# Gated cross-attention with a ternary feed-forward: two subtractions per tile moved from VectorE to GpSimd in the hand-ordered opening, exponential biases made for two banks at a time, dummy matmuls cut into smaller pieces, and the lists of all engines reordered

## What is computed

```python
# x, ctx: 32 tiles of 128 rows x 512; 16 heads of 32
q = rms_norm(linear(layernorm(x), q_w, q_b), norm_q_w)
k = rms_norm(linear(ctx, k_img_w, k_img_b), norm_k_w)     # 128 rows: all of them are "image" rows,
v = linear(ctx, v_img_w, v_img_b)                          # so the text branch is empty
x = x + tanh(g_xattn) * linear(softmax(q k^T / sqrt(32)) v, o_w, o_b)
w1, w2 = ternary(W_fc), ternary(W_proj)                    # sign(w) * group mean |w|, groups of 64, or 0
h = relu(layernorm(x) @ w1.T) ** 2                         # 2048 wide
x = x + tanh(g_ffn) * (rms_norm(h) @ w2.T)
```

## Time and profile before

| | |
|---|---|
| median of 3 runs | 920.4 us (919.91 to 922.21) |
| the profiled execution | 920.16 us, span in the profile 918.3 us |
| busy share of the span | PE 96%, ACT 87%, DVE 77%, POOL 61%, PE weight loads 58% |
| mean granted PE clock | 0.985 of full |
| first maximum (L1640) of tiles 0 to 6 | at 30.28, 56.10, 78.90, 105.53, 134.69, 159.44 and 184.42 us |

### The profile page before, as it was taken

How to read it: one execution, slowest core, us unless ns; L and a number is a source line. 1 busy time by engine, 2 the same in 40 slices (tenths; PEclk the granted TensorE clock), 3 DMA queues, 4 the chain that set the end, 5 groups by cost and what they waited for, 6 DMA issues and landing times.

```text
span 918.3 us, 22391 instructions
## 1 busy us (share of the span) xinstructions
PE 878.6 (96%) x7536; PEld 532.6 (58%) x7633; DVE 710.3 (77%) x1546; ACT 798.8 (87%) x1608; POOL 560.5 (61%) x616
## 2 busy tenths in 40 slices
PE   8687899999999999999999999999999999999998
PEld 5333465555665666656556666555566665556675
DVE  7999999878788787878788787878788787867301
ACT  6998999899899888889989888899898888989573
POOL 3222255776676766667666766667677666656476
PEclk9797899999999999999999999999999999999999
DMA  9958665676676676667666866566667656654501
GB/s 370 208 121 198 147 163 103 100 138 123 127 119 125 127 139 109 106 119 128 127 116 130 132 117 102 119 128 127 120 131 130 116 104 120 124 107 79 82 12 47
DMA packets 319890, 115.78 MB, mean 126 GB/s; under 512 B 305184, under 2 KB 305440, under 8 KB 318240
## 3 DMA queue, kind: packets, MB, share of 16 engines
q1 hardware_dynamic: 319776, 114.34, 63.6%
HBM read 30.67 MB, written 8.39 MB: 43 GB/s over the span
## 4 chain that ended last, share of the span: by engine, by line
PE 76%; ACT 4%; issue 2%; DMA 1%; POOL 1%; DVE 1%; SPq 0%; POOLq 0%; ACTq 0%; DVEq 0%
PE mix_pair L594 11%; PE up_pair L578 10%; PE up_pair L579 10%; PE mix_pair L593 8%; PE score_pair L532 5%; PE score_pair L531 5%; PE score_pair L533 5%; PE mix_pair L531 3%; PE mix_pair L532 3%; PE mix_pair L533 3%; PE score_ps L532 2%; PE score_ps L531 2%; PE score_ps L533 2%; PE score_pair L662 2%; ACT big L1030 1%
## 5 line engine op out<-in xcount | busy, mean ns | idle before, releaser
L578 PE MATMUL up_pair<-ft_all,w 128*128 128x256 f16 x960 | 215.9, 274 | 1.5 <-ACT h_all L1024 0.6
L579 PE MATMUL up_pair<-ft_all,w 128*128 128x256 f16 x960 | 216.0, 274 | 0.0
L2185 POOL TENSOR_TENSOR big<-h_all,big 128x512 f16<-128x512 f32 x128 | 154.2, 1205 | 57.0 <-ACT h_all L1033 38.9
L594 PE MATMUL mix_pair<-w,big 128*128 128x512 bf16 x464 | 175.9, 379 | 7.0 <-issue 4.1
L2195 POOL TENSOR_TENSOR h_all<-h_all,hh_sb 128x512 f32<-128x512 f32 x112 | 143.3, 1279 | 28.1 <-ACT hh_sb L1051 26.7
L593 PE MATMUL mix_pair<-w,big 128*128 128x512 bf16 x383 | 145.2, 379 | 0.2 <-POOL big L2185 0.2
L2140 POOL TENSOR_TENSOR ln_rstd<-ln_in,minus_half 128x1 f32<-128x1 f32 x64 | 46.0, 718 | 112.5 <-issue 90.8
L578 PEld LDWEIGHTS up_pair<-ft_all,w 128*128 128x128 bf16 x960 | 94.0, 98 | 18.4 <-DMA ft_all<-x_rows 1.2
L579 PEld LDWEIGHTS up_pair<-ft_all,w 128*128 128x128 bf16 x960 | 94.1, 98 | 15.8
L1093 ACT ACTIVATE score_ps<-score_ps,exp_bias,exp_scale 128x128 f32<-128x128 f32 x256 | 94.2, 440 | 0.0
L1093 ACT ACTIVATE score_pair<-score_pair,exp_bias,exp_scale 128x128 f32<-128x128 f32 x256 | 93.5, 429 | 0.3 <-DVE exp_bias L1644 0.2
(11 more groups left out here) (236 smaller groups left out, 2304.1 us busy)
## 6 DMA issues: line engine op xcount, KB each, us to landing
x_sb<-in_x SPq DMA_DIRECT2D x32, 256.0 KB, 3.2
ctx_sb<-in_ctx_t SPq DMA_DIRECT2D x32, 256.0 KB, 3.3
out<-out_sb SPq DMA_DIRECT2D x31, 256.0 KB, 3.5
big<-in_w_proj_t SPq DMA_DIRECT2D x4, 1024.0 KB, 5.6
big<-in_w_fc_t SPq DMA_DIRECT2D x2, 1024.0 KB, 7.6
pt<-p_rows SPq DMA_TRANSPOSE x128, 3.2
big<-in_wq_t SPq DMA_DIRECT2D x1, 1024.0 KB, 4.9
big<-in_wk_t SPq DMA_DIRECT2D x1, 1024.0 KB, 7.4
```

What stands on the lines that cost most here:

```text
L578: nc.tensor.matmul(dst[:, half], w, ft[i][:, c, :], start=(c == 0), stop=False)
L579: last = nc.tensor.matmul(dst[:, half], w, ft[i][:, C + c, :], start=False, stop=(c == C - 1))
L594: last = nc.tensor.matmul(dst[:, cols], ht_lo[i][:, row], w2[:, m, cols], start=False, stop=(m == M - 1))
L2185: nc.gpsimd.tensor_tensor(ht_lo[i][:, rows], h_sb[k % 3][:, :], ht_hi[i][:, rows], ALU.subtract).then_inc(hlo_ready, 1)
```

## The change

`x_lo` and `normed_lo` become POOL steps for x_lo(1) to x_lo(7) and normed_lo(0) to normed_lo(4). From tile 6's slot on, DVE does them as before. In the opening, `score_tops` (four times maximum, bias) gives way to `score_tops_by_two` (twice: maximum, maximum, one bias instruction of 8 columns). The dummies: 22 `warm_first` become 16. The 51 `warm` stay 51 but come in calls of 1 or 2 instead of 4 to 6: before scores(1) 9 instead of 14, and 5 between scores(1) and scores(2); between scores(2) and scores(3) 17 instead of 21; between scores(3) and scores(4) 8 instead of 12; between scores(4) and scores(5) 12 instead of 4. All lists of the opening are reordered. The diff, cut to its core:

```diff
@@ SP @@
+            load_context(0, 0)
             load_x(0, 0)
+            load_small(vb_col, v_b, vb_in_ready)
             load_weight(0, wq_t)
-            load_context(0, 0)
...
@@ PE @@
-            warm_first(14)
+            warm_first(5)
+            warm_first(5)
+            spread_context(0, up_b)
             first_rows()
-            spread_context(0, up_b)
-            warm_first(8)
+            warm_first(3)
+            warm_first(3)
...
             ternary_pair(0)
+            scores(0)
             constant_row()
-            scores(0)
+            next_keys(0)
             next_queries(0)
-            next_keys(0)
+            next_values(0)
             values(0)
...
             ffn_up(0, 3, 3, up_ps, 1)
-            next_context(4)
-            ternary_half(31)
-            ffn_down(0, range(0, 4), mix_ps)
+            ffn_up(1, 0, 0, up_b)
+            scores(5)
             ffn_down(0, range(4, 12), mix_ps)
-            scores(5)
             project_out(4)
-            ffn_up(1, 0, 0, up_b)
             square_sums(0)
@@ ACT @@
+            relu(0, 2, 0, up_ps)
             exps(3, 0)
             exps(3, 1)
...
@@ DVE @@
+            def score_tops_by_two(t):
+                dve.wait_ge(s_done, t + 1)
+                if t == 0:
+                    dve.wait_ge(exp_scale_ready, 1)
+                for b in (0, 2):
+                    n, heads = 4 * t + b, slice(4 * b, 4 * b + 8)
+                    need(dve, bias_ready, n - 2)
+                    for i in range(2):
+                        nc.vector.tensor_reduce(m_top[:, 4 * (b + i):4 * (b + i) + 4],
+                                                score_ps[b + i][:, :].rearrange("p (u k) -> p u k", k=P), AX.X,
+                                                ALU.max).then_inc(top_ready, 1)
+                    dve.wait_ge(top_ready, n + 2)
+                    need(dve, exp_ready, n - 2)
+                    nc.vector.tensor_scalar(exp_bias[:, heads], m_top[:, heads], minus_scale[:, :], LOG_P_SCALE,
+                                            ALU.mult, ALU.add).then_inc(bias_ready, 2)
...
-            weight_lo(2)
-            score_tops(0)
+            context_lo(1, 1)
             ternary_clip(0)
             ternary_mask(0)
+            score_tops_by_two(0)
+            weight_lo(2)
             probs_lo(0, 0)
+            constant_row()
             probs_lo(0, 1)
-            context_lo(1, 1)
-            constant_row()
-            weight_lo(3)
+            next_rows(2)
+            k_out(1)
             probs_lo(0, 2)
             probs_lo(0, 3)
@@ POOL @@
+            def x_lo(t):
+                pool.wait_ge(xhi_ready, t)
+                need(pool, xt_in, 16 * (t - 1))
+                nc.gpsimd.tensor_tensor(x_rows[:, 1, :], xn[:, :], x_rows[:, 0, :], ALU.subtract).then_inc(xlo_ready, 1)
+
+            def normed_lo(t):
+                pool.wait_ge(fhi_ready, t + 1)
+                need(pool, ft_in, 16 * t)
+                nc.gpsimd.tensor_tensor(x1_rows[:, 1, :], x1n[:, :], x1_rows[:, 0, :], ALU.subtract).then_inc(flo_ready, 1)
...
             x_norm(1, 1)
+            x_lo(1)
             norm_product()
...
             x1_norm(0, 0)
-            q_norm(2)
+            normed_lo(0)
             x_norm(3, 3)
+            x_lo(3)
...
             k_rms_of(6)
+            rows_plus_constant(4, 0)
+            hidden_lo(1, 0, 0)
             q_norm(6)
```

More of the change, by code:

```diff
@@ L1948, in _ @@
-            q_lo(2)
-            attention(1, 1)
-            ternary_clip(4)
-            ternary_clip(5)
-            ternary_mask(4)
-            ternary_final(3)
-            context_top(3)
-            attention_lo(1)
+            ternary_final(2)
+            probs_lo(1, 2)
+            probs_lo(1, 3)
+            k_out(2)
+            ternary_clip(4)
+            x1_out(0, 0)
+            q_out(2)
+            next_context(3)
+            x1_stats(0, 0)
+            k_lo(2)
+            attention(1, 0)
@@ L1956, in _ @@
+            attention(1, 1)
+            q_lo(2)
+            ternary_mask(4)
+            ternary_signed(4)
+            ternary_final(3)
+            v_lo_of(2)
+            ternary_final(4)
+            ternary_clip(5)
+            ternary_clip(6)
+            ternary_signed(5)
+            attention_lo(1)
+            context_top(3)
+            next_rows(3)
             context_scale(3, 0)
-            ternary_clip(6)
-            normed_lo(0)
-            x_lo(3)
-            ternary_signed(4)
+            score_tops_by_two(2)
@@ L2030, in _ @@
+            v_lo_of(4)
+            ternary_half(25)
+            attention_lo(3)
             k_lo(4)
             context_top(5)
-            next_context(6)
             context_scale(5, 2)
-            q_lo(4)
-            attention_lo(3)
-            x_lo(5)
-            context_lo(5, 1)
-            v_lo_of(4)
-            next_rows(6)
-            ternary_half(27)
-            score_tops(4)
-            probs_lo(4, 0)
-            normed_lo(2)
-            ternary_signed(12)
-            ternary_signed(13)
@@ L2046, in _ @@
-            probs_lo(4, 1)
-            ternary_mask(13)
-            k_out(5)
-            ternary_final(11)
-            probs_lo(4, 2)
-            ternary_half(28)
-            q_out(5)
-            probs_lo(4, 3)
-            ternary_final(12)
-            ternary_final(13)
-            x1_out(3, 3)
+            x1_stats(2, 2)
+            ternary_mask(12)
+            ternary_half(26)
+            next_rows(6)
+            score_tops_by_two(4)
+            ternary_half(27)
+            probs_lo(4, 0)
@@ L2057, in _ @@
+            ternary_final(11)
+            context_lo(5, 1)
+            ternary_mask(13)
+            ternary_signed(12)
+            x1_out(3, 3)
+            probs_lo(4, 1)
+            probs_lo(4, 2)
+            k_out(5)
+            ternary_half(28)
+            probs_lo(4, 3)
+            x1_stats(3, 3)
+            q_out(5)
+            ternary_final(12)
+            ternary_signed(13)
+            k_lo(5)
             ternary_half(29)
-            x1_stats(3, 3)
-            ternary_half(30)
@@ L2094, in _ @@
             attention(5, 1)
+            next_context(7)
             v_lo_of(6)
[L2096 to L2098 removed]
             context_top(7)
             context_scale(7, 1)
+            attention_lo(5)
             for t in range(6, NT - 1):
```

543 lines of the change are left out of this document (272 added, 271 removed).

## The result

The changed kernel takes 923.9 us (median of 21 runs, 921.4 to 926.7), the kernel before 921.3 us beside it (21 runs, 918.9 to 922.9). The ratio is 1.0033 with a 95% interval of 1.0024 to 1.0041. I had forecast 916.7 us. The profiled execution took 921.4 us, which is the fastest of the 21.

A forecast was written before the change was run, and what follows sets the result against it. PE was taken to bound the kernel behind the opening, DVE, then ACT, most of the opening. Stretches -4.3, port +0.3, start -0.7, dummies +1.0 sum to -3.7: 920.4 to 916.7 us, range 911.5 to 922.0.

The forecast's parts named there:

- Start: Before tile 0's first maximum: constant_row behind the scores and a shorter DVE list gain 0.7 us, between 0 and 1.3.
- Four stretches: From tile 0's to tile 4's first maximum: less DVE and ACT work gains 4.3 us, 104.41 becoming 100.1.
- the waits: In the four stretches: time beyond the larger of DVE's and ACT's busy times, kept at 3.9 us.
- the clock: PE behind tile 3's scores: dummies in gaps may lift the low clock; counted 0, gain up to 1 us.
- Subtractions: Six of twelve moves to POOL lie in DVE-bound stretches, 0.60 us each, 3.6 in all; the others count nothing.
- Biases: Two fewer bias instructions per tile save DVE 0.5 us, 2.0 in four stretches; no loss from a later first exponential.
- rival A: Opening: waits between DVE and ACT grow with the relief; gain only 0 to 2.5 us, about 919.3 us; chance 0.22.
- Port: Opening: a busier POOL slows a few short DVE instructions over the shared port, +0.3 us, between 0 and 7.0.
- Rival D: Each moved subtraction on POOL blocks DVE for its whole length, 7.0 us instead of 0.3: 923.4 us; chance 0.03.
- Dummies: Last two stretches before tile 6: eight more dummies and q_norm(6) behind more POOL steps cost 1.0 us, between 0 and 3.
- rival C: POOL becomes a tile's late link, delaying tiles 3 to 6; at 2 us each 924.7 us; chance 0.10.

The follow-up runs named there:

- e9: The changed kernel with only the rows of tile 0 ahead of the context again, in loads, DVE's list and PE's list: 923.7 us, ratio 1.0029.
- e5: The changed kernel with the whole old start and context_hi(1, 1) on ACT moved ahead of the third weight's high half: 918.5 us, ratio 0.9968.
- e14: The same kernel as e5, run again for a trace: 919.5 us, ratio 0.9984 to the kernel before.
- e13: The changed kernel itself, run again for a second trace: 925.5 us, ratio 1.0050, with the trace from a run of 926.0 us.
- e3: The changed kernel with only x_lo(1) moved back from POOL to DVE: 924.1 us, ratio 1.0033.
- e10: The kernel of e5 with the biases of tiles 0 to 5 a bank at a time again (score_tops): 923.1 us, ratio 1.0030.
- e6: The changed kernel with all twelve moved subtractions back on DVE: 931.6 us, ratio 1.0111.
- e8: The kernel before with only the biases of tiles 0 to 5 computed for two banks at once: 922.9 us, ratio 1.0024.
- e7: The kernel before with only the twelve subtractions moved to POOL: 926.0 us, ratio 1.0053.
- e11: The kernel of e5 with 4 instead of 12 dummies between the scores of tiles 4 and 5: 919.3 us, ratio 0.9983.
- e2: The changed kernel with only the order of the first loads as before: 928.6 us, ratio 1.0076.
- e15: The kernel of e14 with 12 instead of 2 of the last dummies ahead of tile 3's scores: 917.2 us, ratio 0.9961.

## Why the prediction was wrong

The step that failed is *Start*: "I take 0.7 us, between 0 and 1.3. The order of the first loads and `constants` behind `context_max` I take at 0, with 1 us either way, since the 1 MB weight and its absolute sum are still to come." It measured +3.1 us at tile 0's mark, outside both bounds. The reason I gave is the error. I followed the weight to the first projection and not the other input, the rows: their statistics, norm, transposes and copy. In the kernel before the copy is done by 7.7 us and the first projection starts at 9.99: a slack of some 2.3 us. The norm is now 3.5 us later and the copy 4.0, and the dummies and the weight's spread stand behind the transposes on PE, so they are late with it. e9 puts only the rows first again and brings 2.3 of the 3.1 us back at the mark. With the whole start as before (e5, e14) the ratios make the rest of the change worth -2.9 and -1.5 us, where my sum without the start says -3.0.

*Four stretches*, -4.3: with the port, -4.0 against -2.8 in the first trace. The larger of DVE's and ACT's busy times adds up to 97.0 us there instead of the forecast 96.2, and the waits to 4.6 instead of 3.9. In the run of 926.0 us (e13) the four take 103.70 us, -0.7. I called the clock "0, the gain can reach 1". Between these two traces the third and fourth stretch differ by 2.1 us, in part by the clock, and the fifth by 2.5, by a late transposing DMA with a low clock behind it. I had no term for a difference between runs of one program. This is the second failure, and a part of why undoing 3.2 us of start gives 4.4 to 6.0: e3's and e13's traces have the long fifth stretch, e14's has not.

In the difference of the medians I was off by 6.3 us (-3.7 forecast, +2.6 measured). Of this 3.8 is the start and 1.5 the other stretches of the first trace; the rest is mostly that the median run is 2.5 us slower than that trace, against 1.1 us in the kernel before.

*Subtractions.* Six at 0.60 in bound stretches and nothing for the others is too little for the others: e10 loses 2.1 us to DVE in the fifth stretch alone, and e6 6.6 in the last two, its places being a part of that. *Biases.* The 2.0 us is a gain in the changed lists (e10: 3.6 to 4.6) and a loss in the old ones (e8: 1.8). My argument "ACT's list has other work queued before it" holds for the one and not for the other. What I wrote under rival A, that ACT is not busy for 3 us per stretch, misread my own rows: it is 1.0 to 2.4 us.

*Port*, 0.3 us within 0 to 7.0: the size was off. DVE's groups in the changed kernel from 0 to 185 us:

```profile
L1646 DVE TENSOR_TENSOR w<-w,abs_w 128x1024 bf16<-128x1024 bf16 x16 | 11.9, 750 | 0.1
L1618 DVE TENSOR_TENSOR abs_w<-abs_w,out_sb 128x1024 bf16<-128x1024 bf16 x11 | 8.1, 742 | 0.0
L1467 DVE TENSOR_TENSOR at_rows<-pt,at_rows 128x512 f16<-128x512 f32 x6 | 4.6, 770 | 0.1
L1530 DVE SCALAR_TENSOR_TENSOR q_rows<-q_raw,q_rms,q_rows 128x512 f16<-128x512 f32 x7 | 5.9, 843 | 0.0
```

Before they took 684, 684, 684 and 790 ns in the mean, and so 2.6 us less together. The means hide what happens: most of these instructions keep their length, and a few take up to 1.3 us, each time when POOL had started an instruction shortly before. Two such meetings in the changed kernel, DVE's instruction and then POOL's:

```profile
132.00 1.31 DVE L1618 TENSOR_TENSOR abs_w<-abs_w,out_sb 128x1024 bf16<-128x1024 bf16 x1
131.49 1.27 POOL L2218 TENSOR_TENSOR h_all<-h_all,hh_sb 128x512 f32<-128x512 f32 x1
184.49 1.22 DVE L1467 TENSOR_TENSOR at_rows<-pt,at_rows 128x512 f16<-128x512 f32 x1
184.01 1.16 POOL L2238 TENSOR_TENSOR x_rows<-xn,x_rows 128x512 f16<-128x512 f32 x1
```

In both DVE's instruction ends 0.55 us after POOL's. The second is one of the moved subtractions, the first is not. e7 has its `w` and `abs_w` products with `out_sb` at 685 and 683 ns, but `at_rows` at 877 and `q_rows` at 913; e6, with no subtraction on POOL, has `abs_w` back at 685, `w` only at 727 and `at_rows` at 1092. So it is which instructions meet that counts, in POOL's other work as well. Rival D, a whole subtraction blocking DVE each time, did not come. The Trainium skill (SBUF — State Buffer, on the port pair of VectorE and GpSimd) says that whichever of the two starts first holds the pair for its whole instruction and the other waits. The traces agree on both sides: DVE waits in the two rows above, and POOL's subtraction takes 2.88 us for 1.16 where DVE had started first.

*Dummies*, +1.0: the last two stretches gave +1.27 in the first trace, and PE is busy there for 1.5 us more than before (49.55 against 48.04), as priced; e11's trace takes 1.4 of PE's time back. What the term lacks is the other thing that can happen there: SP issues the transposes of tile 3's rows right behind POOL's `normed_lo(3)` (153.99 and 154.01 us in the first trace), PE waits for them, and behind the longest waits the clock falls (e2, e3, e13). That is rival C in a mild form, at tile 5 only.

One reading of mine was wrong without changing the sum. The tile "from 184.42 to 209.50 us" does not end at a mark: tile 7's is at 210.50, and a tile of the loop takes 26.1 to 26.2 us, not 25.1, before and after the change.

Still open: why the transposing DMA of tile 3's rows lands after 3.3 us in some runs and after 4.9 in others, and so the fifth stretch takes 25.9 or 28.4 us; and why the end behind tile 31's mark takes 78.0 to 80.2.

The fastest kernel found is e15: the changed kernel with the old start, `context_hi(1, 1)` early and ten dummies more. It takes 917.2 us, 0.39% less than the kernel before (five runs).

## What to carry to other kernels

When a change reorders the first loads, follow every input of the first large step on every engine, and ask which one has no slack; an in-order list that asks for data in one order while a queue brings it in another can cost more than either order alone (928.6 us in e2). Parts of a change that was laid out as a whole can't be priced by taking them alone: three of three lost time in the old lists and two of them gained in the new. Where TensorE waits for a transfer ahead of its main work, price the clock behind the gap as well as the gap, and try filling it up to a little less than its length. And when one program's runs scatter by as much as the effect, take a second trace before reading a cause out of the first.

## What the runs showed of the hardware

- TensorE's clock was granted at 0.72 or at 1.00 in the same window of the same program in two runs (e13 and the first trace). At the lower level the 128x256 matmuls started 0.21 us apart instead of 0.11. The length of the wait ahead did not decide it alone: behind 3.0 us it was 1.00 in e14 and 0.73 in e11. Ten dummies more in the gap (1.6 us of work) brought the median down by 2.3 and 4.6 us.
- A POOL subtraction of 128x512 f32 took 2.88 us instead of 1.16 while DVE ran a 2.35 us instruction with two SBUF inputs; a product there took 2.22 instead of 1.27. DVE's instruction kept its 2.35 us. Where POOL had started first it was DVE that took longer: 1.31 and 1.22 us instead of 0.69.
- The same transposing DMA took 3.3 us from issue to landing in one run and 4.9 in another of the same program. PE's wait for it was 0.5 and 2.1 us, and the granted clock in the 5 us from 160 us on 1.00 and 0.68.
- The loop of identical tiles took 601.5 us from tile 8's mark to tile 31's in every trace; the code behind it, the same in all, took 78.0 to 80.2 us.
